# A two-layer decoder kernel: the first layer's orders on all engines, and its out product with the two batches' split rests in turn

## What is computed

```python
# attention of layer 0, per batch
q, k, v = (conv4(h @ W) for W in (Wq, Wk, Wv))      # causal depthwise convolution, 6 heads of 64
angles from q and k; alpha = sigmoid(h @ Wa); beta = sigmoid(h @ Wb)
state = rotate(state, phi) * alpha + beta * rotate(v, psi)   # a scan over the 512 tokens
o = rms(rotate(state, -theta)) * rms_w * silu(h @ Wg)
x = x + o @ Wo
# feed-forward of layer 0
s = sigmoid(h @ centroids.T) + gate_bias            # 16 experts, the best two of each token
x = x + 0.1 * shared_swiglu(h) + sum of the two chosen experts' swiglu, weighted
```

## Time and profile before

| | us |
|---|---|
| median of 3 runs (lowest to highest) | 2190.09 (2186.99 to 2191.32) |
| the profiled execution's own time | 2186.43 |
| its span, first to last instruction | 2184.7 |
| unit 0's products, until pass y = 1 starts | 68.2 |
| passes y = 1, 2, 3 | 115.9, 106.1, 102.5 |
| last unit alone | 97.3 |
| experts and layer 1 | 1694.7 |

### The profile page before, as it was taken

One profiled execution on the slowest core, in us unless ns is written; L12 is line 12 of the kernel. 1 busy time (PEld: TensorE's weight loads), 2 busy tenths in 40 slices (PEclk: granted clock), 3 DMA queues, 4 the chain that ended last, 5 costly groups with the idle time before them and its releaser, 6 DMA issues. The chain is left out here.

```text
span 2184.7 us, 36727 instructions
## 1 busy us (share of the span) xinstructions
PE 2094.5 (96%) x12638; PEld 1820.3 (83%) x12638; DVE 1631.5 (75%) x4282; ACT 1239.6 (57%) x3432; POOL 590.9 (27%) x624
## 2 busy tenths in 40 slices
PE   6789898979999999999999999999999999999997
PEld 5667676858778999899889989998998999899897
DVE  6657675888868887777876777787677778767775
ACT  4434333126667667666666666666566566656662
POOL 3313333530505223213221322322132222222220
PEclk9989899999999999999999999999999999999999
DMA  9111211337532112112112211211221121111100
GB/s 317 39 34 48 66 41 54 141 120 216 171 110 73 45 54 73 41 53 73 49 42 61 73 40 54 71 51 40 62 75 40 54 69 54 39 58 50 40 20 20
DMA packets 92840, 154.56 MB, mean 71 GB/s; under 512 B 8688, under 2 KB 56560, under 8 KB 92656
## 3 DMA queue, kind: packets, MB, share of 16 engines
q1 hardware_dynamic: 72192, 121.53, 18.8%
q0 software_dynamic: 6144, 16.79, 2.3%
q10 hardware_dynamic: 14320, 13.90, 1.9%
HBM read 112.85 MB, written 39.32 MB: 70 GB/s over the span
## 5 line engine op out<-in xcount | busy, mean ns | idle before, releaser
L714 POOL TENSOR_TENSOR wo_low<-wraw_o,wo_high 128x256 fp32r<-128x256 f32 x128 | 95.1, 743 | 1141.0 <-ACT wo_high L778 1141.0
L1088 ACT ACTIVATE pr<-bank,negmax 128x128 f32<-128x128 f32 (+3 forms) x512 | 263.5, 527 | 195.6 <-DVE negmax L1647 195.6
L1208 DVE TENSOR_TENSOR p_low<-bank,p_high 128x512 fp32r<-128x512 f32 (+2 forms) x384 | 190.3, 551 | 101.1 <-ACT p_high L778 100.3
L778 ACT ACTIVATE p_high<-bank 128x512 fp32r<-128x512 f32 (+2 forms) x384 | 177.5, 497 | 149.4 <-PE bank L2206 149.4
L1647 DVE CUSTOM_DVE_ANT_0 bank<-bank,causal 128x128 f32<-128x128 f32 (+3 forms) x512 | 234.8, 521 | 1.1 <-PE bank L1834 1.1
L1674 DVE SCALAR_TENSOR_TENSOR xs<-bank,rinv,xs 128x256 f32<-128x256 f32 x512 | 211.8, 476 | 1.2 <-PE bank L1834 1.2
L1832 PE MATMUL bank<-h_high,wqk_high 128*128 128x512 f32 x512 | 202.5, 396 | 0.2 <-DVE h_low L1208 0.2
L1834 PE MATMUL bank<-h_high,wqk_low 128*128 128x512 f32 x512 | 202.4, 395 | 0.0
L1833 PE MATMUL bank<-h_low,wqk_high 128*128 128x512 f32 x512 | 202.4, 395 | 0.0
L1208 DVE TENSOR_TENSOR z_low<-bank,z_high 128x512 fp32r<-128x512 f32 x128 | 88.5, 691 | 130.8 <-ACT z_high L778 130.4
L704 POOL TENSOR_TENSOR wqk_low<-wraw,wqk_high 128x512 fp32r<-128x512 f32 x128 | 166.1, 1298 | 0.1
(11 more groups left out here) (350 smaller groups left out, 6198.4 us busy)
## 6 DMA issues: line engine op xcount, KB each, us to landing
wraw<-in_wpair SPq DMA_DIRECT2D x64, 512.0 KB, 4.0
wraw<-in_wpair SPq DMA_DIRECT2D x64, 256.0 KB, 4.4
wraw_o<-in_wpair SPq DMA_DIRECT2D x64, 256.0 KB, 2.9
tokens_by_expert<-xm SPq DMA_DIRECT2D x10, 1024.0 KB, 10.9
xt<-tokens_by_expert SPq DMA_DIRECT2D x40, 256.0 KB, 3.2
expert_results<-ey ACTq DMA_DIRECT2D x40, 256.0 KB, 3.7
wres<-in_wexp SPq DMA_DIRECT2D x1, 6144.0 KB, 19.8
xs<-x_between_stages SPq DMA_DIRECT2D x8, 512.0 KB, 4.8
```

Of the source, the lines that this page charges most:

```text
L714: pool.tensor_tensor(wo2[e][1][:], wraw_o[r][:, e, :], wo2[e][0][:].bitcast(F32), ALU.subtract).then_inc(s_wo, 1)
L778: sc.activation(dst, src, ACT.Copy, scale=scale).then_inc(done, 1)
L1088: ins = sc.activation(pr[:, i, 0:(i + 1) * P], score(i), ACT.Exp, scale=-1.0, bias=negmax[:, i:i + 1], accum_out=rsum[:, i:i + 1])
L1208: v.tensor_tensor(at(parts[1]), src, high_, ALU.subtract).then_inc(done, 1)
```

## The change

It alters the orders of layer 0 on all engines and leaves the amount of arithmetic nearly as it is.

- PE: the products for alpha and beta come first among the gate products (`GATES` reordered) and ahead of `value_products(y, 0)`; `square_sums(x, 2)` comes between the two halves of `value_products(y, 1)`; `out_products` does the full rows of both batches first, each group as soon as its gated row is there, and then the rests of the two batches in turn; `router_turn` is split around `value_products(y, 2)` and loses its wait and its 6 turns of the identity; `router_ranks` writes bank 3; `first_turn` stands between the two `shared_down`.
- ACT: `alpha_beta` first; the normalising of the two batches is split and takes the first once its statistics are there.
- DVE: `rms` ahead of `angle_sum`, the gating ahead of both halves of `conv_value(y, 1)`, layer norm statistics per batch (two chains of 17 instructions for one), `shared_product` and `router_picks` in another order.
- SP: the clearing of the sorted list goes behind the first spreading; `be` is read ahead of `al`, each with its own wait.

```diff
-        GATES = ((6, 0), (7, 0), (6, 1), (7, 1), (6, 2), (7, 2), (8, 0), (8, 1))
+        GATES = ((8, 0), (8, 1), (6, 0), (7, 0), (6, 1), (7, 1), (6, 2), (7, 2))
...
+        def ranks_of(u):
+            return bank[0 if u == NU - 1 else 3]
...
-            sp.wait_ge(s_hl, 4)
-            for n in range(NTILE // 8):
-                sp.dma_start(xsort[n * 8 * P:(n + 1) * 8 * P, :]...
...
-                if u >= 1:
-                    sp.wait_ge(s_scan, RT * u)
-                    sp.wait_ge(s_bm, RT * u)
-                for q, dst in enumerate((al, be)):
+                for q, dst, used in ((1, be, s_bm), (0, al, s_scan)):
+                    if u >= 1:
+                        sp.wait_ge(used, RT * u)
...
             spread_alpha_beta(0)
+            for n in range(NTILE // 8):
+                sp.dma_start(xsort[n * 8 * P:(n + 1) * 8 * P, :]...
...
 # ACT, the loop over y
+                whole_turns(y, 0)
+                alpha_beta(y)
                 tap_value(y, 0)
-                gates(y, (0, 1))
                 squares(x, 0)
-                whole_turns(y, 0)
                 gates(y, (2, 3))
                 gates(y, (4, 5))
                 squares(x, 1)
-                alpha_beta(y)
+                gates(y, (6, 7))
                 sin_cos(y, 0)
...
-                router_norm(x)
+                router_norm_part(x, 0)
                 whole_turns(y, 2)
+                router_norm_part(x, 1)
+                router_input(x, (0, 1))
                 tap_value(y, 2)
-                router_input(x)
+                router_input(x, (2, 3))
...
 # DVE, the loop over y
+                rms(x)
                 angle_sum(y)
-                rms(x)
-                conv_value(y, 1, (0,))
                 for r in range(RT):
                     gated(x, r)
-                conv_value(y, 1, (1,))
+                conv_value(y, 1)
                 reduce_angle(y, 1)
                 for ab in range(2):
                     residual(x, ab)
                     unit_stats(1, xu[x % 3], ab)
-                unit_norm(1, s_ln2)
+                    unit_norm(1, s_ln2, slice(ab * NT, (ab + 1) * NT))
...
 # PE
+            def out_products(u):
+                gates_of = (ge[u % 2], go[u % 2])
+                for ab in range(2):
+                    if ab == 1:
+                        pe.wait_ge(s_y, RT * u + RT)
+                        pe.wait_ge(s_gr, NG0 * (u + 1) + NG0)
+                    for i in range(NT):
+                        if ab == 0 and i % 2 == 0:
+                            pe.wait_ge(s_y, RT * u + 1 + i // 2)
+                        for par, src in enumerate(gates_of):
+                            mm(dst(ab, i), src[:, 2 * ab, i * P:(i + 1) * P], wo_all[:, par, :],
+                               start=(i % 2 == 0 and par == 0), stop=False)
+                for i in range(NT):
+                    for par, src in enumerate(gates_of):
+                        for ab in range(2):
+                            half = slice(ab * P // 2, (ab + 1) * P // 2)
+                            ins = mm(dst(ab, i), src[half, SPLIT_ROW, i * P:(i + 1) * P], wo_rest[half, par, :],
+                                     start=False, stop=(i % 2 == 1 and par == 1))
...
 # PE, the loop over y
                 angle_products(y, 0)
                 pe.wait_ge(s_hl, 4 * y + 4)
+                gate_products(y, (0, 1))
                 value_products(y, 0)
-                gate_products(y, (0, 1, 2, 3))
+                gate_products(y, (2, 3))
                 square_sums(x, 0)
-                gate_products(y, (4, 5))
+                gate_products(y, (4, 5, 6, 7))
                 square_sums(x, 1)
-                gate_products(y, (6, 7))
                 angle_products(y, 1)
+                value_products(y, 1, (0,))
                 square_sums(x, 2)
-                value_products(y, 1)
+                value_products(y, 1, (1,))
                 for r in range(RT):
                     rms_turn(x, r)
-                for ab in range(2):
-                    out_product(x, ab)
+                out_products(x)
                 angle_products(y, 2)
+                router_turn(x, 0)
                 value_products(y, 2)
-                router_turn(x)
+                router_turn(x, 1)
...
                     shared_gate_up(x, 2)
+                    shared_gate_up(x, 3)
                     router_ranks(x)
+                    shared_down(x, 0)
+                    first_turn(y + 1)
+                    shared_down(x, 1)
```

More of the change, by code:

```diff
@@ L922, in _ @@
             input_high(0)
+            alpha_beta(0)
             tap_value(0, 0)
-            gates(0, (0, 1))
+            gates(0, (2, 3))
             sc.wait_ge(s_setup, SETUP)
             high(quantities(w8[0], 0, 4), taps_raw.rearrange("p k s n -> p k (s n)"), s_w8h)
-            gates(0, (2, 3))
+            gates(0, (4, 5))
             whole_turns(0, 0)
@@ L930, in _ @@
             unit_apply(1, 0, xu[1], xn1, s_xn1, s_ln1)
-            gates(0, (4, 5))
+            gates(0, (6, 7))
             sin_cos(0, 0)
             angle_copy(0)
-            alpha_beta(0)
             whole_turns(0, 1)
@@ L1391, in places @@
                     v.wait_ge(s_p0, u * ROUTER_LINKS)
[L1392 to L1393 removed]
+                ranks = ranks_of(u)[:, 0:UT * NEXP].rearrange("p (t e) -> p t e", t=UT)
+                totals = ranks_of(u)[:, UT * NEXP:(UT + 1) * NEXP]
                 v.scalar_tensor_tensor(place[:], ranks, 1.0 / P, spread(fill[old]), ALU.mult, ALU.add)
@@ L1524, in _ @@
                     unit_stats(1, xu[x % 3], ab)
-                unit_norm(1, s_ln2)
+                    unit_norm(1, s_ln2, slice(ab * NT, (ab + 1) * NT))
                 reduce_angle(y, 2)
-                conv_value(y, 2)
                 if y + 1 < NU:
                     first_stats(y + 1)
-                    logits_clamped(x)
+                conv_value(y, 2, (0,))
+                logits_clamped(x)
+                conv_value(y, 2, (1,))
+                if y + 1 < NU:
                     unit_norm(0, s_ln1)
                     shared_product(x, 0)
+                    shared_product(x, 1)
                     router_picks(x)
+                    shared_product(x, 2)
+                    places(x)
                 else:
-                    logits_clamped(x)
                     router_picks(x)
                     shared_product(x, 0)
-                shared_product(x, 1)
-                places(x)
-                shared_product(x, 2)
+                    shared_product(x, 1)
+                    places(x)
+                    shared_product(x, 2)
                 shared_product(x, 3)
@@ L1849, in unit_turn @@
                     for k in range(KD):
+                        if done is s_t1 and (ab, k) == (1, KD - 1) and u >= 2:
+                            pe.wait_ge(s_slot, u - 1)
                         for i in range(NT):
@@ L1896, in alpha_beta_product, with value_products @@
                 return ins
-            def value_products(u, r):
-                for j in range(2):
+            def value_products(u, r, halves=(0, 1)):
+                for j in halves:
                     if RT * u + r >= 1:
@@ L2009, in router_ranks @@
                 if u + 1 < NU:
-                    pe.wait_ge(s_as, u + 2)
+                    pe.wait_ge(s_cb[1], RT * (u + 2))
                 pe.wait_ge(s_pk, u + 1)
                 chosen = picks[:].rearrange("p t e -> p (t e)")
-                mm(bank[0][:, 0:UT * NEXP], before[:], chosen, start=True, stop=False)
+                ranks = ranks_of(u)
+                mm(ranks[:, 0:UT * NEXP], before[:], chosen, start=True, stop=False)
                 for i in range(1, UT):
-                    mm(bank[0][:, i * NEXP:UT * NEXP], all_bf[:], chosen[:, 0:(UT - i) * NEXP], start=False,
+                    mm(ranks[:, i * NEXP:UT * NEXP], all_bf[:], chosen[:, 0:(UT - i) * NEXP], start=False,
                        stop=(i == UT - 1))
                 for i in range(UT):
-                    ins = mm(bank[0][:, UT * NEXP:(UT + 1) * NEXP], all_bf[:], picks[:, i, :], start=(i == 0),
+                    ins = mm(ranks[:, UT * NEXP:(UT + 1) * NEXP], all_bf[:], picks[:, i, :], start=(i == 0),
                              stop=(i == UT - 1))
@@ L2089, in _ @@
                     shared_gate_up(x, 2)
-                shared_gate_up(x, 3)
-                if y + 1 < NU:
-                    first_turn(y + 1)
-                for ab in range(2):
-                    shared_down(x, ab)
+                    shared_gate_up(x, 3)
+                    for ab in range(2):
+                        shared_down(x, ab)
             x = NU - 1
```

64 lines of the change are left out of this document (20 added, 44 removed).

## The result

The changed kernel took 2151.31 us (median of 4 runs, 2149.97 to 2151.93) against 2190.7 for the kernel before on the same chip: ratio 0.982, 95% interval 0.9803 to 0.9837. The profiled execution took 2151.93 with a span of 2150.2, so its span is 34.5 shorter than that of before.

What follows compares the result with a forecast made beforehand. PE was taken as the bound, by its work and its waits. Gains of 14.0 + 4.2 + 1.2 (passes), 0.8 (unit 0) and 4.35 (pairing) made 24.5 us: 2186.4 to 2161.9, plus 3.7 for the median, 2165.5; range 2154 to 2180.

Steps and rivals of the forecast that it cites:

- The full-clock schedule with paired rests: Passes without low clock: 97.6, 97.6 and 97.0 us serial, less 3.7, 2.5 and 2.5 if the rests pair.
- Clock: Loss to low PE clock in each of three passes: 4.3 us, half of what y = 2 lost, bounds 1.7 and 8.5.
- Norm and router turn: Out product to gate-up: both batches end together, new PE waits on `xm`; gate-up at T = 74.5 serial, 72.0 paired (y = 2, 3).
- The weight of the pairing: Out product's rests at once on two array halves: worth 8.7 us over three passes, half of it, 4.35, counted.
- the serial schedule: Rests one after another, 7.3 us: out product ends at T = 55.1 and gate-up starts at T = 74.5.
- five handovers: Chain before the out product: semaphores and engine drains, estimated 0.14 each, 0.7 us in its start at T = 40.5.
- the wait on the gate's read: PE's 7.9 us wait in y = 1, from unit 0's late alpha and beta, would go; that pass gains 14.0.
- the scatter that holds `xm` in y = 2 and 3: If the rests pair, ACT's `xm` waits for the last scatter of unit y - 2, landing near T = 61.2.
- the ranks' wait: End of pass y = 3, which has no `first_turn`: a wait of 1.2 us before the ranks.
- More: Rival, chance 0.07: clock never falls and the rests pair, 41.8 us gained, so 2148.
- The gain was not eaten: Rival, chance 0.10: rests cost as now or 1.6 more, clock loses 8.5 as before; 2182.5 to 2187.3 us.
- TensorE did not stay at 1.2 GHz: Rival, chance 0.05: half clock from the root's transposes to gate-up's end, 25.5 us lost three times; about 2229.

Runs made afterwards that it cites:

- e4: Changed kernel with 18 (y = 1) or 46 (y = 2, 3) identity transposes filling PE's wait on `xm` before the first router turn: 2148.3 us, ratio 0.9801.
- e11: Changed kernel with identity transposes in three waits: before the root's transposes, the first router turn and, in y = 1, the second: ratio 0.9792.
- e1: Changed kernel with the rests of batch 0 first, then those of batch 1, nothing else: 2149.2 us, ratio 0.9806.
- e8: Changed kernel with the out product as before: batch 0 whole, then batch 1, behind the gating of all three rows: ratio 0.9815.
- e12: Changed kernel with the out product batch by batch (full rows, then rests, of each), still starting from the first gated row: 2143.4 us, ratio 0.9785.
- e5: Changed kernel with the chain from the squares to the gating put back as before: 2148.8 us, ratio 0.9814.
- e2: Kernel before with only the alpha-beta part: its products and readings first, list clearing behind the first spreading, beta read before alpha: 2171.7 us, ratio 0.9926.
- e9: Kernel before with the alpha-beta part and statistics, `xm` and transposes batch by batch, identity turns dropped: ratio 0.9844, again 0.9859 (2159.6 us).
- e10: Changed kernel with the end of a pass in the old order on TensorE and VectorE in y = 1 and 2: ratio 0.9813.
- e13: Changed kernel with out product batch by batch, all scatters ahead of the beta steps, identity transposes before the root's transposes: 2155.1 us, ratio 0.9843.
- e3: Changed kernel with GpSimd's 16 scatters of unit y - 2 all ahead of the three beta steps: 2151.7 us, ratio 0.9812.
- e7: Kernel before, nothing of the change, with identity transposes in three waits per pass: 2184.5 us, ratio 0.9975.

## Why the prediction was off, step by step

By spans the forecast was a gain of 24.5 and 34.5 was found. The other 4.3 us of the miss of 14.2 have nothing to do with the change: I took the median of the kernel after to lie 3.7 above its profiled execution, as before, and it lay 0.6 below. Unit 0 ends within some 6 us from one execution to the next, and the profiled one of before was a short one.

The 10.0 us of the spans lie in three terms of the sum. The full-clock schedule with paired rests gave 93.9 + 95.1 + 94.5 = 283.5 for the passes, and 288.8 was found. I had added 12.9 for the clock and 4.35 for half of the pairing; so 12.0 came from the passes, less 1.9 in the last unit and behind it. They split so:

- *"Clock", 3.4 us too much.* The forecast took half of 25.8 us of low clock, 12.9. The low time was nearly that, 23.8; its price was not half. Without low clock the passes of this order take 93.0 and 92.9 (e4; the 3.4 us that the second still had cost next to nothing there) and 93.4 in y = 1 (an estimate: e11's 95.1 less half of its 3.4). So the changed kernel lost 4.4 + 2.7 + 2.4 = 9.5 to the clock, 0.4 of its low time, since part of a low stretch lies in the wait ahead of the work.
- *"Norm and router turn", 4.2 too much:* 93.4 + 93.0 + 92.9 = 279.3 against the 283.5 of the schedule. At full clock gate-up comes at T = 69.9 in y = 2, not 72.0. Of these 2.1, 1.5 are the last scatter (ACT's `xm` at 59.7, forecast 61.2); the other 0.6 lie between `xm` and gate-up, where the short waits on the copies are not there.
- *The weight of the pairing, 4.35.* The rests did pair, at the lower bound of 3.65. I sized this as 3.7 + 2.5 + 2.5 on the path and took half. But e1, e8 and e12 show that the pairs are worth nothing on this path, so even the model behind the term failed, and what was too dear is the serial schedule that they were to be measured against: it had gate-up at T = 74.5, and e1, with its rests one batch after the other, reaches it at T = 70.0 in y = 2. My serial case had the rests still alternating, both batches late together; kept batch by batch they start the norm of the first batch sooner. No run has rests that alternate without pairing, so the 74.5 itself is not measured.

So the step that failed is the schedule from the out product to gate-up: it put 4.2 us too much on the new order and priced the pairs against a serial order whose gate-up comes 4.5 us later in y = 2 than that of the serial kernel e1. The clock's price is the other term.

The 0.7 us for five handovers in the start of the out product stood on no row. In pass y = 2 of the changed kernel they took some 0.5 together, and the out product started at T = 40.0 where 40.5 was forecast.

Right were the direction, the end of the wait on the gate's read and pass y = 1 like the others, beta at 54.06 (forecast near 54), the out product's start, the pairing in the trace, the scatter that holds `xm` in y = 2 and 3, the ranks' wait of 1.3 in y = 3 (1.2), the clearing that costs nothing. Unit 0's 0.7 against 0.8 is luck: the same kernel's profiles differ there by up to 6.7. For the start of the out product the total was right and its sharing was not: e5 shows that root and gating ahead of the convolution give 2.7 us and the half of the value products put ahead of the sums takes 2.4 back; what counts is the squares' wait (e2, 2.5 us) and the start from the first gated row (e8, 2.3 us). Of the rivals, *More* (2148) was nearest. Its pairs were right in the trace but not in their worth, and its clock that never falls was not right: clock took 9.5 us. That its 2148 came near is in good part luck. The gain was not eaten and TensorE did not stay at 1.2 GHz: passes had a granted clock of 0.95 and 0.96.

What stays open: how much of the 9 us of e9 to the changed kernel belongs to which part, since no single one accounts for it. The traces say where they lie: from gate-up to the end of a pass, added over the three passes, e9 takes 76.3 and 77.1 us, the changed kernel 70.6, 70.8 and 73.3, so 3 to 6 of the 9 are in the end of the pass. There e9 waits for the ranks and the places; in its y = 2:

```profile
254.48 0.22 PE L2003 MATMUL bank<-picks,before 128*128 128x128 bf16 x1 [1.73 <-DVE picks L1365]
...
259.83 1.97 PE L1844 MATMUL bank<-ident,xn 128*128 128x128 f32 x16 [1.15 <-DVE slots L1403]
```

Why the same order of the end costs at most 2.4 in e10 is not shown. For y = 2 it is shown that the clock falls with the wait on `xm` (e4, e12); what lets it fall in y = 1 is not.

## What to carry to other kernels

Faster matmuls in front of a wait only lengthen it, and here the longer wait cost clock as well. Before two streams of products are interleaved, look at what the first of them feeds: here the batch that ends early covers the chain of the other, and batch by batch from the first ready row on beats pairs at twice the rate by 5 to 7 us. Where several parts of a change each undo to nothing, build up from the kernel before as well (e2, e9): only that showed that two parts of five carry 27 of the 36 us. Compare stages, not only totals, when the head of a kernel varies by more than the effect, and profile the same kernel more than once: here its three passes are known to 2 us.

## What the runs showed of the hardware

- GpSimd holds VectorE up over several instructions. A 128x4 `TENSOR_SCALAR` on SBUF took 5.48 us instead of 0.17 and ended with the last of four `TENSOR_TENSOR` of 128x512 in a row on GpSimd (e13); in its y = 3 a 128x4 `TENSOR_TENSOR` took 5.60, and in e3 one took 2.60, through two of GpSimd's. (The Trainium skill, SBUF — State Buffer, Who interferes with whom, says that a VectorE instruction with two inputs in SBUF, or in a two-port mode, contends with GpSimd for a shared port pair, and that whoever issues first holds it for the whole instruction while the other blocks fully; the trace agrees on the blocking, and adds that VectorE did not get in between GpSimd's four. Whether the `TENSOR_SCALAR` ran in a two-port mode no trace here shows.)
- Two f32 matmuls of 64 rows on the two halves of the array and into different banks ran at twice the rate: 32 records in 3.66 us, 16 in 3.65.
- In pass y = 2 of the changed kernel the granted clock fell to 1.2 GHz during a wait of 5.2 us; with that wait filled by transposes of the identity it stayed at 2.4 GHz (e4), and with a wait of 1.4 too (e12). The low time cost some 0.4 of its length: 2.5 us for a stretch of 6.8 (e4), some 10 for 24 (e7).
